# One transformer block on one core: a bias product in two halves, and another order in the last unit and the last products

## What is computed

```python
mod = (silu(c) @ wmod).reshape(2, 6, 1, 256)          # sa, ca, ga, sb, cb, gb
ga, gb = (2 * (g >= 0) - 1) * maximum(abs(g), 0.25)   # for both gates
h = layernorm(x) * (1 + ca) + sa
q, k, v = (h @ W + bias, 16 heads of 128)             # q scaled; q and k get the rotary embedding
x = x + ga * (softmax(causal(q @ k.T)) @ v @ Wo + bo)
h = layernorm(x) * (1 + cb) + sb
x = x + gb * down(silu(gate(h)) * up(h))              # hidden 704, weights (int - 128) * scale
```

## Time and profile before

| | us |
|---|---|
| median of 3 runs (lowest, highest) | 1036.28 (1036.2, 1036.66) |
| the profiled execution | 1035.97 |
| its span | 1034.2 |
| PE busy in it | 1006.3 (97%) |
| DVE busy | 771.6 (75%) |
| ACT busy | 678.5 (66%) |
| POOL busy | 620.3 (60%) |

### The profile page before, as it was taken

How to read it: one execution, slowest core, us unless ns; L and a number is a source line. 1 busy time by engine, 2 the same in 40 slices (tenths; PEclk the granted TensorE clock), 3 DMA queues, 4 the chain that set the end, 5 groups by cost and what they waited for, 6 DMA issues and landing times.

```text
span 1034.2 us, 20453 instructions
## 1 busy us (share of the span) xinstructions
PE 1006.3 (97%) x6318; PEld 903.9 (87%) x6318; DVE 771.6 (75%) x1664; ACT 678.5 (66%) x1447; POOL 620.3 (60%) x472
## 2 busy tenths in 40 slices
PE   6989999999999999999999999999999999997997
PEld 5878999899989999999988999999999999986786
DVE  6668887777777877877777777777787777887644
ACT  5766766666666666666667666666666667767763
POOL 3365665666565755576555765665656655675654
PEclk9999999999999999999999999999999999999999
DMA  8412111211112211211112111221122113221011
GB/s 253 120 41 70 44 32 42 72 44 38 37 35 71 51 41 32 67 44 41 41 43 60 41 41 42 71 51 31 32 70 51 41 37 91 62 62 42 1 42 43
DMA packets 41987, 56.03 MB, mean 54 GB/s; under 512 B 5508, under 2 KB 25028, under 8 KB 41924
## 3 DMA queue, kind: packets, MB, share of 16 engines
q1 hardware_dynamic: 41924, 55.37, 20.8%
HBM read 19.69 MB, written 2.10 MB: 21 GB/s over the span
## 4 chain that ended last, share of the span: by engine, by line
PE 91%; DVE 2%; issue 2%; ACT 2%; POOL 1%; DMA 1%; SPq 0%; DVEq 0%; ACTq 0%; POOLq 0%
PE ps_r L1362 18%; PE ps_r L1361 18%; PE ps_r L1360 17%; PE ps_t L1519 12%; PE ps_s L1362 7%; PE ps_s L1361 7%; PE ps_s L1360 6%; PE ps_s L1367 2%; PE ps_s L1370 1%; PE ps_r L1369 1%; PE ps_r L1367 1%; PE ps_r L1458 1%; DMA wmod_a<-in_L_wmod 1%; POOL y L695 0%; ACT probs L907 0%
## 5 line engine op out<-in xcount | busy, mean ns | idle before, releaser
L651 POOL TENSOR_TENSOR swapped<-swapped,sin_sb 128x512 f32<-128x512 f32 x124 | 166.1, 1340 | 236.1 <-DMA swapped<-straight 235.6
L896 ACT ACTIVATE pT_hi<-ps_t 128x512 fp32r<-128x512 f32 (+3 forms) x384 | 186.8, 491 | 85.2 <-PE ps_t L1519 83.1
L1198 DVE TENSOR_TENSOR pT_lo<-ps_t,pT_hi 128x512 fp32r<-128x512 f32 (+3 forms) x384 | 202.3, 550 | 53.7 <-ACT pT_hi L896 53.6
L1263 DVE CUSTOM_DVE_ANT_0 ps_s<-ps_s,mask_wide 128x128 f32<-128x128 f32 (+7 forms) x256 | 194.5, 760 | 55.8 <-PE ps_s L1362 41.6
L661 POOL TENSOR_TENSOR qk_lo<-straight,qk_hi 128x512 fp32r<-128x512 f32 x124 | 162.2, 1322 | 112.3 <-ACT qk_hi L802 112.3
L907 ACT ACTIVATE probs<-ps_s,neg_max 128x128 f32<-128x128 f32 (+7 forms) x256 | 190.3, 743 | 44.1 <-DVE neg_max L1263 37.0
L1519 PE MATMUL ps_t<-ident,probs 128*128 128x128 f32 x1152 | 185.6, 274 | 6.5 <-DVE pT_lo L1198 5.9
L652 POOL TENSOR_TENSOR straight<-straight,cos_sb 128x512 f32<-128x512 f32 x124 | 180.9, 1459 | 0.0
L1126 DVE TENSOR_TENSOR straight<-straight,swapped 128x512 f32<-128x512 f32 x126 | 129.1, 1025 | 32.5 <-POOL straight L652 32.0
L1519 PEld LDWEIGHTS ps_t<-ident,probs 128*128 128x128 f32 x1152 | 134.3, 140 | 11.3 <-issue 4.9
L1360 PE MATMUL ps_s<-qk_hi 128*128 128x512 f32 (+3 forms) x384 | 139.9, 364 | 0.1
(11 more groups left out here) (195 smaller groups left out, 2221.1 us busy)
## 6 DMA issues: line engine op xcount, KB each, us to landing
swapped<-straight SPq DMA_DIRECT2D x252, 128.0 KB, 2.3
x_in<-in_L_attn_x SPq DMA_DIRECT2D x4, 512.0 KB, 5.5
w_raw<-in_L_attn_Wk SPq DMA_DIRECT2D x8, 256.0 KB, 3.3
w_raw<-in_L_attn_Wq SPq DMA_DIRECT2D x8, 256.0 KB, 3.5
w_raw<-in_L_attn_Wv SPq DMA_DIRECT2D x8, 256.0 KB, 3.6
wo_all<-in_L_attn_Wo SPq DMA_DIRECT2D x1, 2048.0 KB, 9.9
wo_raw<-in_L_attn_Wo SPq DMA_DIRECT2D x8, 256.0 KB, 2.7
x<-in_L_attn_x SPq DMA_DIRECT2D x4, 512.0 KB, 4.1
```

The costliest lines, as they stand in the source:

```text
L651: pool.tensor_tensor(swapped[:, q, :], swapped[:, q, :], sin_sb[:, cs], ALU.mult)
L896: nc.scalar.activation(turned_at(ORDER[step], k0, k1)(pT_hi), ps_t[:, (T_FIRST[step] + j) % 2, 0:(k1 - k0) * P].rearrange("p (k q) -> p k ...
L1198: nc.vector.tensor_tensor(turned_at(t, k0, k1)(pT_lo), ps_t[:, (T_FIRST[step] + j) % 2, 0:(k1 - k0) * P].rearrange("p (k q) -> p k q", q=P ...
L1263: nc.vector.tensor_tensor_reduce(rows, rows, mask_wide[:, SEQ - n_keys:SEQ], -1.0, -MASKED, ALU.add, ALU.min, accum_out=neg_max[:, t:t + 1 ...
```

## The change

The bias product becomes two pieces, B0 with heads 0 to 7 and B1 with heads 8 to 15, with turns 0.0 and 1.0 between them; the second sum adds to row 0 of y, and everything that waited for the bias counts to 2. The lists of unit 0 on ACT and DVE are put in another order around it. The exponential of step 3 of unit 0 no longer waits for turned blocks, and DVE waits for its own last h low half before it writes the first blocks of step 1. In unit 31 the down pieces D0 to D2 come before W10 and W11, the sums move later on DVE, and the last sum of unit 30 into the list of the ending; the third down copy on POOL moves ahead of a gate of rows. In the feed-forward stage xn2 groups 4 and 5 are turned and output at n = 8 and 9 instead of 7 and 8, and POOL's low halves come at 9 and 10 instead of both at 8. The last low part (n = 23) is made by DVE instead of POOL. The last down product does tiles 0 to 2 with parts 0 to 3, then with 4 and 5, and then tile 3.

```diff
 
 NORMAL_AT = {6: 2}
 EARLY_NORMAL_AT = {9: 3}
-TURN_AT = {7: (4,), 8: (5,), 13: (6,), 14: (7,)}
-LOW_AT = {0: (2,), 1: (3,), 8: (4, 5), 14: (6,), 15: (7,)}
+TURN_AT = {8: (4,), 9: (5,), 13: (6,), 14: (7,)}
+LOW_AT = {0: (2,), 1: (3,), 9: (4,), 10: (5,), 14: (6,), 15: (7,)}
 PAUSE_AT = {1: 1}
 
 OUT_TILES = [(2 * n, 2) for n in range(NTT // 2 - 2)] + [(n, 1) for n in range(NTT - 4, NTT)]
@@ -96,13 +96,12 @@
 
 PLANS_0 = {
     TENSOR_PLAN: """make:P0- make:P1- mods:1 scores:0 xn:4 make:K0+ xn:5 scores:1 make:Q0+ xn:6 xn:7 scores:2 scores:3
-        make:B turn:0.0 turn:1.0 scores:4 turn:1.1 make:K1+ turn:2.0 scores:5 make:Q1+ turn:3.0 turn:3.1 make:V0
+        make:B0 turn:0.0 turn:1.0 make:B1 scores:4 turn:1.1 make:K1+ turn:2.0 scores:5 make:Q1+ turn:3.0 turn:3.1 make:V0
         turn:4.0 scores:6 make:V1 turn:5.0 scores:7 turn:5.1""",
-    SCALAR_PLAN: """exp:0 out:K0+ xout:4 xout:5 exp:1 out:Q0+ xout:6 xout:7 exp:2 exp:3 high:K0+ high:Q0+ turn:0.0
-        turn:1.0 exp:4 turn:1.1 out:K1+ turn:2.0 exp:5 out:Q1+ turn:3.0
-        turn:3.1 turn:4.0 high:V0 high:K1+ high:V1 turn:5.0 exp:6 split:O turn:5.1 high:Q1+""",
-    VECTOR_PLAN: """max:0 max:1 xlow:4 xlow:5 max:2 max:3 add:K0+ xlow:6 xlow:7 add:Q0+ sum:B turn:0.0
-        turn:1.0 max:4 turn:1.1 gates:0 turn:2.0 max:5 turn:3.0 add:K1+ turn:3.1
+    SCALAR_PLAN: """exp:0 out:K0+ xout:4 xout:5 exp:1 out:Q0+ xout:6 xout:7 exp:2 turn:0.0 exp:3 turn:1.0 high:K0+ high:Q0+
+        turn:1.1 exp:4 out:K1+ turn:2.0 turn:3.0 exp:5 turn:3.1 out:Q1+ turn:4.0 high:V0 high:K1+ high:V1 turn:5.0 exp:6 split:O turn:5.1 high:Q1+""",
+    VECTOR_PLAN: """max:0 max:1 xlow:4 xlow:5 max:2 max:3 add:K0+ xlow:6 xlow:7 turn:0.0 sum:B0 turn:1.0 add:Q0+ sum:B1
+        turn:1.1 max:4 gates:0 turn:2.0 max:5 turn:3.0 add:K1+ turn:3.1
         turn:4.0 max:6 low:V0 low:V1 add:Q1+ max:7 turn:5.0 turn:5.1""",
     POOL_PLAN: """rotate:K0+ rotate:Q0+ low:K0+ low:Q0+ rotate:K1+ rotate:Q1+ low:K1+ low:Q1+ bias:0 split:O"""}
 
@@ -123,13 +122,13 @@
 PLANS_31 = {
     TENSOR_PLAN: """make:K0+ make:Q0+ scores:0 turn:6.0- turn:7.0- scores:1 scores:2 turn:7.1- make:P0- turn:0.0
         make:P1- scores:3 turn:1.0 make:W00- make:X scores:4 turn:1.1 turn:2.0 make:W01- scores:5 make:D0 turn:3.0
-        make:W10- turn:3.1 turn:4.0 make:W11- scores:6 make:D1 turn:5.0 scores:7 make:D2 turn:5.1""",
+        make:D1 turn:3.1 scores:6 make:D2 turn:4.0 make:W10- scores:7 turn:5.0 make:W11- turn:5.1""",
     SCALAR_PLAN: """out:K0+ exp:7- turn:6.0- exp:0 out:Q0+ turn:7.0- turn:7.1- high:P0- turn:0.0 exp:1 exp:2
-        high:P1- turn:1.0 turn:1.1 exp:3 turn:2.0 exp:4 gated:0 out:D0 turn:3.0
-        exp:5 turn:3.1 turn:4.0 out:D1 exp:6 turn:5.0 out:D2 turn:5.1""",
+        high:P1- turn:1.0 turn:1.1 exp:3 turn:2.0 exp:4 gated:0 turn:3.0 out:D0
+        exp:5 turn:3.1 out:D1 turn:4.0 out:D2 exp:6 turn:5.0 turn:5.1""",
     VECTOR_PLAN: """largest:3 max:0 turn:6.0- turn:7.0- turn:7.1- max:1 low:P0- max:2 turn:0.0 moments:0
-        low:P1- max:3 sum:W00- turn:1.0 width:X max:4 turn:1.1 turn:2.0 sum:W01- max:5 turn:3.0 sum:W10- turn:3.1 turn:4.0
-        sum:W11- max:6 max:7 turn:5.0 turn:5.1"""}
+        low:P1- max:3 turn:1.0 sum:W00- width:X max:4 turn:1.1 turn:2.0 max:5 sum:W01- turn:3.0 turn:3.1
+        max:6 turn:4.0 max:7 turn:5.0 sum:W10- turn:5.1"""}
 
 
 ENDING = {
@@ -138,7 +137,7 @@
     SCALAR_PLAN: """exp:7- turn:6.0- turn:7.0- turn:7.1- silu_table:0 high:P0- normal:0 normal:1 normal:2 normal:3
         normal:4 normal:5 normal:6 normal:7 high:P1- h2out:0 h2out:1 h2out:2 silu:0 h2out:3 silu:1 gu:0 silu:2 gu:1 silu:3 gu:2
         silu:4 gu:3 silu:5 gu:4""",
-    VECTOR_PLAN: """turn:6.0- turn:7.0- turn:7.1- moments:1 newton:0 low:P0- low:P1- sum:W00- sum:W01-
+    VECTOR_PLAN: """turn:6.0- turn:7.0- turn:7.1- sum:W11-- moments:1 newton:0 low:P0- low:P1- sum:W00- sum:W01-
         sum:W10- sum:W11- moments:2 ffn:0 ffn:1 moments:3 ffn:2 newton:2 ffn:3 ffn:4 ffn:5"""}
 UNIT_29 = {SCALAR_PLAN: """out:K0+ exp:7- turn:6.0- exp:0 out:Q0+ turn:7.0- turn:7.1- high:P0- turn:0.0 exp:1 float:0 exp:2
         high:P1- high:K0+ high:Q0+ turn:1.0 float:1 out:K1+ turn:1.1 exp:3 turn:2.0 exp:4 out:Q1+ float:2 turn:3.0
@@ -158,7 +157,7 @@
     plan = last.get(u, {}).get(plan, plan)
     for token in plan.split():
         what, name = token.rstrip("+-").split(":")
-        v = u + {"+": 1, "-": -1}.get(token[-1], 0)
+        v = u + token.count("+") - token.count("-")
         if what == "split":
             which = "QKVO".index(name)
             n = v // UNITS + (which != WO)
@@ -679,7 +678,7 @@
                         qk_low(ps, piece)
                     elif what == "bias":
 
-                        pool.wait_ge(attn_bias_ready, 1)
+                        pool.wait_ge(attn_bias_ready, 2)
                         pool.tensor_copy(y[:, 1:NTT, :], y[:, 0, None, :].broadcast_to([P, NTT - 1, DIM])).then_inc(y_added, 1)
                     else:
                         w_low(x, ps.passes(piece))
@@ -742,9 +741,9 @@
             gate_wo_low()
             down_high(0)
             down_high(1)
+            down_high(2)
             pool.wait_ge(y_added, 1 + 4 * (ALL_UNITS - 1))
             gate_rows(2)
-            down_high(2)
             pool.wait_ge(rstd2_ready, 1)
             gate_rows(3)
             add_rows(2, 6)
@@ -760,6 +759,8 @@
                     pool.wait_ge(rstd2_ready, PAUSE_AT[n] + 1)
                 pool.wait_ge(gu_hi_ready, n + 1)
                 low = gu_lo[:, n % GU, :]
+                if n == NCH * HM - 1:
+                    break
                 if size == HLAST:
 
                     low = gu_hi[HLAST:P, n % GU, :]
@@ -901,7 +902,7 @@
             def exponentials(ps, u, step):
                 t = ORDER[step]
                 act.wait_ge(max_ready, ps.tiles(u, step + 1))
-                if u * NQ + step >= 3:
+                if u * NQ + step > 3:
 
                     act.wait_ge(turned, ps.groups(*divmod(u * NQ + step - 2, NQ)))
                 nc.scalar.activation(probs[:, P_AT[step] * P:(P_AT[step] + t + 1) * P], ps_s[:, step % 2, 0:(t + 1) * P],
@@ -1175,7 +1176,11 @@
             def bias_row(ps, piece):
                 dve.wait_ge(piece_made, ps.pieces(piece))
                 dve.wait_ge(wo_all_ready, 32)
-                nc.vector.tensor_tensor(y[:, 0, :], ps_r[:, ps.bank(piece), 0:DIM], bo_wide[:, :], ALU.add)\
+                more = bo_wide[:, :]
+                if piece[1] == 1:
+                    dve.wait_ge(attn_bias_ready, 1)
+                    more = y[:, 0, :]
+                nc.vector.tensor_tensor(y[:, 0, :], ps_r[:, ps.bank(piece), 0:DIM], more, ALU.add)\
                     .then_inc(attn_bias_ready, 1)
 
             def gate_columns():
@@ -1194,6 +1199,9 @@
 
                 t = ORDER[step]
                 k0, k1 = groups_of(t)[j]
+                if u * T_UNIT + T_FIRST[step] + j == T_FIRST[1]:
+
+                    dve.wait_ge(hT_ready, GROUPS4)
                 dve.wait_ge(pT_hi_ready, ps.groups(u, step, j + 1))
                 nc.vector.tensor_tensor(
                     turned_at(t, k0, k1)(pT_lo),
@@ -1347,6 +1355,11 @@
                     dve.wait_ge(g_ready, 2)
                     dve.wait_ge(down_made, j + 1)
                     finish(2 * j, 2, ps_r[:, j % 2, :].rearrange("p (t n) -> p t n", t=2))
+            last = NCH * HM - 1
+            dve.wait_ge(gu_hi_ready, last + 1)
+            dve.wait_ge(gu_split, last)
+            nc.vector.tensor_tensor(gu_hi[HLAST:P, last % GU, :], gu_at(last, HLAST),
+                                    gu_hi[0:HLAST, last % GU, :].bitcast(F32), ALU.subtract).then_inc(gu_split, 1)
             for j in range(4):
                 dve.wait_ge(down_made, (NCH - 1) * 2 + j + 1)
                 finish(NTT - 4 + j, 1, (ps_r, ps_t)[j // 2][:, j % 2, None, 0:DIM])
@@ -1389,7 +1402,7 @@
                 elif old[0] == "width":
                     pe.wait_ge(wide_ready, 1)
                 elif old[0] == "bias":
-                    pe.wait_ge(attn_bias_ready, 1)
+                    pe.wait_ge(attn_bias_ready, old[1] + 1)
                 else:
                     pe.wait_ge(y_added, ps.rank(old, 2))
 
@@ -1454,9 +1467,10 @@
                             ins = nc.tensor.transpose(dst[:, at_:at_ + P], f_down[:, k, m * P:m * P + P], ident[:, :])
                 elif piece[0] == "bias":
                     pe.wait_ge(wo_all_ready, 32)
-                    for h in range(HEADS):
+                    half = HEADS // 2
+                    for h in range(piece[1] * half, piece[1] * half + half):
                         ins = nc.tensor.matmul(dst[:, 0:DIM], cols[:, COL_BV + h:COL_BV + h + 1].broadcast_to([P, P]),
-                                               wo_all[:, h, :], start=h == 0, stop=h == HEADS - 1)
+                                               wo_all[:, h, :], start=h % half == 0, stop=h % half == half - 1)
                 elif piece[0] == "width":
```

(11 more changed lines are left out.)

## The result

The changed kernel takes **1040.11 us** (median of 7 runs, 1038.18 to 1042.31) against 1036.2 of the kernel before on the same chip: ratio 1.004, 95% interval 1.0028 to 1.0052. It is 3.9 us slower, where +1.4 was forecast, and above the range, which ended at 1039.6. The profiled execution took 1042.31 us with a span of 1040.4. It is the slowest of the seven, 2.2 us over their median, so what it shows can be more than what the median pays.

What follows compares the result with a forecast made beforehand. TensorE, 91% of the span, was taken as the bound, so only its idle time counts. -1.2 + 1.4 + 2.4 - 1.15 = +1.4 us on the median 1036.28 gave 1037.7 us, range 1034.4 to 1039.6.

Steps and rivals of the forecast that it cites:

- unit 0 and last products: Start and end of kernel: halved bias removes two PE waits, -1.2 us; DVE's finishes start earlier, -1.15 us.
- unit 31 and the ending: New DVE order delays the moments of x, so the first feed-forward product starts +1.4 us late; bounds +0.8 and +2.0.
- tables, at full clock: Feed-forward: 0.78 us wait before block 4 goes, but PE stands about 3.2 us before product 12; sum +2.4 us.
- the clock: Granted clock in the stand before product 12: a fall could not be excluded, but none was counted in the sum.
- rival: 1.5, chance 0.25: Clock falls in the stand before product 12; products at half speed cost 1.5 us, giving 1039.2; chance 0.25.
- part of 3.3 us at turns 5.0 and 6.0: Unit 0: PE gives back 2.1 of 3.3 us, about 1.2 at turn 5.0, the rest ahead of turn 6.0.
- The sum in front of the moments: Ending: the sum of W11 (0.8 us) on DVE makes the moments start at 948.0 instead of 946.58.
- D1's wait for W01's sum: Unit 31: D1 takes W01's PSUM bank and must wait for its sum, so PE stands 1.2 us.
- the sentence on the gate of rows 2: Ending: POOL's gate, 948.1 to 950.5, waits for the moved sum but is hidden by 2 us of POOL waiting.
- first feed-forward product 0.2 us later: Sign of being right: that product starts 0.2 us later than before on the axis (-1.2 + 1.4).
- The queue of four POOL operations: Feed-forward: split 8, low 4, split 9, low 5 on POOL, 988.0 to 993.2; product 12 waits for low 5.
- The rival's condition, a gap over 2.4 us: The clock falls before product 12 if PE's gap is over 2.4 us; that decides the slower case, chance 0.25.

Runs made afterwards that it cites:

- e1: Changed kernel with unit 31, the ending, the third down copy and both feed-forward tables as before, keeping unit 0 and the last products: 1033.97 us.
- e2: Changed kernel with only the two feed-forward tables as before (blocks 4 and 5 turned at 7 and 8, both low halves at 8): 1036.13 us.
- e4: Changed kernel plus ten idle-filling matmuls on PE just before its wait for product 12: 1037.95 us.
- e3: Changed kernel with only the lists of unit 31 and the ending, and the third down copy, as before: 1037.46 us.
- e10: Kernel of e1 with blocks 4 and 5 both turned at 8, and DVE's low half of block 3.1 ahead of K1's add in unit 0: 1032.95 us.
- e6: Kernel before with only the unit 0 part of the change (bias in two pieces, its lists and waits): 1034.62 us.
- e8: Kernel of e4 plus ten more idle-filling matmuls before the first turned block of the normalised x in the ending: 1037.9 us.
- e7: Kernel before with only the last products changed (tile order, last low part on DVE): 1035.15 us.

## Why the prediction was wrong

| step | forecast | measured (medians) | from |
|---|---|---|---|
| unit 0 and last products | -1.2 - 1.15 | -2.3 | e1 |
| unit 31 and the ending | +1.4 | +2.2 | e2 - e1 |
| tables, at full clock | +2.4 | +1.8 | e4 - e2 |
| the clock | 0 (rival: 1.5, chance 0.25) | +2.2 | changed - e4 |
| sum | +1.4 | +3.9 | |

Each measured step is the difference of two neighbours, so that they add up to 3.9 is no proof. Another pair is one: with unit 31 as before, the tables and their clock cost 3.5 us (e3 - e1), with unit 31 changed 4.0 (changed - e2). If the tables alone cost 1.8, the clock is 1.7 or 2.2 us.

- **Unit 0: right**, place and mechanism. Both waits went, PE gave back part of 3.3 us at turns 5.0 and 6.0, and e10 shows that the rotation holds it. The size varied: in the changed kernel's profile turn 6.0 is 1.45 us earlier (as is the output of Q1 on ACT, 58.55 against 60.00) and unit 31 0.95, and e6's median shows 1.75; the forecast was 1.2.
- **Unit 31: right in the path, but one wait was missing: 0.8 us short in size,** just past its upper bound of 2.0. The sum in front of the moments and D1's wait for W01's sum came as written (1.08 us for 1.2; moments 1.5 us late for 1.4). The term that was missing is in the sentence on the gate of rows 2: I priced it only as POOL's time and found it "hidden by the 2 us in which POOL waits for the roots". It is hidden on POOL, but it runs beside DVE's variances and holds them for 0.57 us. So the sign "first feed-forward product 0.2 us later" failed too: it was 0.65 us later in e2, at full clock, and 1.86 in the changed kernel's profile. The row of before that would have warned me was there: DVE's add took 1.77 us beside POOL against 0.69 undisturbed. It started at 66.19, POOL's subtraction had begun at 66.12 and ended at 67.41, and the add ended 0.54 us after that.
- **Tables: right.** The queue of four POOL operations and the stand (3.10 us for a forecast 3.2) came as written; the 0.78 us were won. From the product that follows PE's wait of 0.9 us near 972 to product 18 it is 2.1 us at full clock (37.67 us in e8, 35.57 in e2), for +2.4 forecast.
- **Last products: right**, -1.1 in the trace and -1.2 alone.
- **The clock: this is the step that failed.** I named the mechanism, the place and the level, and left it out of the sum because "idle times up to 1.8 us inside the kernel did not bring it down". That says nothing of a wait of 3.2 us. The only row near that length was the fall at 1030.40, 2.4 us after PE's last product, and it spoke for a fall. The Trainium skill, page "TensorE: Matmul & The Clock Gate", section "Why this matters for your kernels", which I had cited, warned of exactly such a gap; the runs agree with it, 0.50 after waits of 3.10 and 3.09 us in both profiles that had them unfilled. I should have had the fall in the forecast, at about 1039.2. The rival's condition, a gap over 2.4 us, was not the right one either: the clock also fell after 2.25 and 2.21 us. Its price of 1.5 us let part of the slow stretch pass under the wait. In e3's profile none of it did, and the 3.4 us cost 1.55 us (39.22 us from the same product, near 970 there, to product 18, against 37.67 in e8 with the clock at 1.00). In the changed kernel's profile 5.7 us at half speed cost 2.6 (40.25 us). The medians show 1.7 (e3) and 2.2 us (changed kernel).

What stays open: what decides, around a wait of 2.2 us, whether the clock falls. It fell in the profiles of the changed kernel and of e4, 0.9 and 0.4 us after PE had begun to work again, and not in that of e2, with the same instructions around it. Open too is why the low level lasts 3.4 us in some executions and 6.8 in others, and how often each comes: only one execution of each kernel has a profile.

## What to carry to other kernels

An idle time of PE of some 3 us can cost more than its length: here 2.2 us on top of 3.1, and ten products that nobody needs, put in the gap, won them back. Where work is moved onto an engine that idles, look at what its neighbour does at that moment: a gate of 2.4 us on POOL held a DVE operation of 0.17 us on the critical chain. And when one entry of an order table is moved past an entry that waits for another engine, everything behind it waits too: turning block 4 a product later won 1.1 us, and with block 5 and the two low halves moved on as well the same tables cost 1.8 us even at full clock.

## What the runs showed that was not expected

DVE's 128x4 operation on the variances (one SBUF input, fp32) takes 0.17 us, and 0.74 us when it comes while POOL's tensor operation runs: it ended at 949.61 where POOL's ended at 949.59 in the changed kernel, and at 949.27 for 949.25 in e2. The moments and their aggregation before it, beside the same POOL operation, took 1.39 and 0.38 us as ever. So it is a wait to the end of the other's instruction, not a slower pace, and not every DVE operation is subject to it. The Trainium skill, page "SBUF — State Buffer", section "SBUF: two separate sides", describes the port pair shared by the two engines as a lock held for the whole instruction; the trace agrees.

The low clock in the ending, which I had put at 1.4 us from one profile, was worth 0.9 us even there and nothing that can be seen in the medians (e4 against e8). That profile is 2.2 us above its median, and three places in it make up most of that: the 0.9 us in the ending, 0.4 us more behind product 12 than the medians show for the clock (2.6 against 2.2), and at the end a tail of 4.0 us, where e1 has 3.2 and e7 3.6. One more of the seven runs took as long (1042.29), and whether it did so in the same places no trace shows.
